# Query and key halves of a three-phase attention kernel, through DRAM into head order

## The reference

```python
x = x + 0.5 * ffn(norm(x))        # softmax attention and experts
x = x + linear_attention(norm(x)) # elu + 1 features, causal
x = x + 0.5 * ffn(norm(x))        # the same weights again

def ffn(x):                       # 16 heads of 8, 8 experts, top 2
    h = layernorm(x, ln1);  q, k, v = h @ wq, h @ wk, h @ wv
    scores = where(causal, q @ k.T, -inf)
    x = x + softmax(scores / sqrt(8)) @ v @ wo + bo
    h = layernorm(x, ln2);  top 2 of h @ gate_w, softmax over the two
    return x + sum over the two of weight * (silu(h @ w1) * (h @ w2)) @ w3

def linear_attention(x):
    q, k = elu(x @ Wq.T) + 1, elu(x @ Wk.T) + 1;  v = x @ Wv.T
    kv, ks = cumsum(k outer v), cumsum(k)         # per head, over tokens
    return (q . kv / max(q . ks, 1e-6)) @ Wo.T
```

## Time and profile before

| | |
|---|---|
| median of 3 runs | 1413.6 us (1412.59 to 1418.59) |
| the profiled execution | 1418.66 us, span 1416.9 us |
| mean granted clock of TensorE | 0.912 of full speed |
| busy in the span | TensorE 77%, VectorE 79%, ScalarE 59%, GpSimd 39% |
| SyncE's queue | 72.68 MB, 17.7% of the time of 16 DMA engines |

### The profile page before, as it was taken

How to read it: one execution, slowest core, us unless ns; L and a number is a source line. 1 busy time by engine, 2 the same in 40 slices (tenths; PEclk the granted TensorE clock), 3 DMA queues, 4 the chain that set the end, 5 groups by cost and what they waited for, 6 DMA issues and landing times.

```text
span 1416.9 us, 37025 instructions
## 1 busy us (share of the span) xinstructions
PE 1085.8 (77%) x12412; PEld 819.6 (58%) x12412; DVE 1115.8 (79%) x2411; ACT 839.7 (59%) x1311; POOL 548.4 (39%) x681
## 2 busy tenths in 40 slices
PE   4688888888854998476877868989888888549980
PEld 3566666666643666255655546857666666436660
DVE  6868889999965887677577767779999999658875
ACT  2457777777843555244656544668777787535550
POOL 6620255555563666201000004002555555636661
PEclk9899999999966999688999987999999999769995
DMA  8911111111102332201033310011111111023326
GB/s 292 412 48 38 43 46 49 51 43 51 53 20 61 86 90 69 82 30 34 7 77 79 79 43 19 0 28 45 50 49 45 51 53 47 26 57 88 87 72 187
DMA packets 124880, 98.71 MB, mean 70 GB/s; under 512 B 41584, under 2 KB 116848, under 8 KB 124784
## 3 DMA queue, kind: packets, MB, share of 16 engines
q1 hardware_dynamic: 103216, 72.68, 17.7%
q0 software_dynamic: 9088, 18.76, 4.0%
q10 hardware_dynamic: 12480, 6.02, 1.5%
HBM read 24.61 MB, written 40.94 MB: 46 GB/s over the span
## 4 chain that ended last, share of the span: by engine, by line
DVE 29%; PE 24%; issue 20%; ACT 9%; POOL 6%; DMA 6%; SPq 3%; DVEq 1%; ACTq 1%; POOLq 0%
DVE negm L1058 6%; PE banks L311 4%; POOL ys L1464 4%; SPq L1552 3%; PE banks L293 3%; DVE p_lo L1277 2%; DMA kst<-k_all 2%; DVE negm L1062 2%; ACT pf L866 2%; DVE pf L1284 2%; DVE x_all L1017 2%; PE banks L434 2%; ACT p_hi L732 2%; PE banks L430 2%; PE banks L466 2%
## 5 line engine op out<-in xcount | busy, mean ns | idle before, releaser
L715 ACT ACTIVATE pf<-banks 128x1536 f32<-128x1536 f32 x128 | 185.7, 1451 | 121.0 <-PE banks L455 119.9
L1070 DVE TENSOR_TENSOR p_lo<-pf,p_hi 128x1536 f16<-128x1536 f32 x128 | 223.9, 1749 | 3.2 <-ACT p_hi L732 3.0
L1464 POOL DMA_INDIRECT ys<-q_all,dest x156 | 151.4, 970 | 115.8 <-ACT q_all L872 90.9
L732 ACT CAST p_hi<-pf 128x1536 f16<-128x1536 f32 x128 | 188.7, 1474 | 2.0
L1415 POOL DMA_INDIRECT xs<-n_all,slot x128 | 164.7, 1287 | 54.9 <-issue 37.6
L1058 DVE TENSOR_REDUCE negm<-banks 128x4 f16<-128x1024 f32 x128 | 156.0, 1219 | 28.7 <-PE banks L434 20.3
L1441 POOL TENSOR_SCALAR rs<-mv 128x2 f32<-128x2 f32 x32 | 44.3, 1385 | 346.0 <-DVE mv L1113 295.3
L455 PEld LDWEIGHTS banks<-ident,negm 128*128 128x128 f16 x1536 | 119.7, 99 | 78.1 <-issue 4.4
L455 PE MATMUL banks<-ident,negm 128*128 128x128 f16 x1536 | 150.1, 221 | 0.0
L448 PE MATMUL banks<-qst,kst 128*128 128x512 f16 x384 | 148.1, 386 | 2.1 <-ACT pf L715 2.1
L434 PE MATMUL banks<-kst,qst 128*128 128x128 f16 x1536 | 129.7, 221 | 0.0
(11 more groups left out here) (206 smaller groups left out, 2820.9 us busy)
## 6 DMA issues: line engine op xcount, KB each, us to landing
xs<-qst SPq DMA_DIRECT2D x20, 975.0 KB, 25.4
qst<-q_all SPq DMA_DIRECT2D x384, 32.0 KB
q_all<-xs SPq DMA_DIRECT2D x78, 130.0 KB
kst<-k_all SPq DMA_DIRECT2D x66, 128.0 KB
pf<-ys SPq DMA_DIRECT2D x32, 256.0 KB, 3.0
v_hl<-v_all SPq DMA_DIRECT2D x66, 68.0 KB, 2.1
kst<-k_all ACTq DMA_DIRECT2D x30, 128.0 KB
ys<-q_all,dest POOLq DMA_INDIRECT x156
```

What stands on the lines that cost most here:

```text
L715: nc.scalar.activation(pf[:, g % 2, :, :, :].rearrange(flat), banks_t[:, :, :].rearrange("p a b -> p (a b)"), ACT.Exp, scale=HD ** -0.5).t ...
L732: nc.scalar.copy(p_hi[:, g % 2, :, :, :].rearrange(flat), pf[:, g % 2, :, :, :].rearrange(flat))\
L1070: nc.vector.tensor_tensor(lo, pf[:, g % 2, :, :, :].rearrange(flat), hi, ALU.subtract)\
L1464: nc.gpsimd.indirect_dma_start(ys, bass.IndirectOffsetOnAxis(ap=dest[:, t % YB, h:h + 1], axis=0), y_out[:, t % YB, h, :], None).then_inc( ...
```

## The change

The selection matrices, `front_spread`, its evacuations, `q_all` and `k_all` are removed. A DRAM tensor `qk_d` takes their place, with the rows in head order. SyncE stores each batch's high and low halves to it in six DMAs of 64 KB, as soon as `qk_low` is done; `qk_hi` and `qk_lo` have three buffers, and ScalarE's `qk_high` waits until the store of three batches before has landed. `load` brings a whole batch back in six DMAs (four of queries, one of keys, one of values) into one of three places (`RB = 3`) of `qst`, `kst` and `v_hl`. TensorE waits for a batch as a whole (`batch_in`), and SyncE loads batch b when batch b - 3 is finished.

The order in SyncE's queue is: all 16 stores of a phase, then the loads of batches 0, 1, 2, then in the first phase w3 (`load_w3`) and the clears (`clear_rows`, from a new buffer `zeros`), then the other loads. In the linear phase loads of the experts' results are placed between the stores, and ScalarE issues no DMA any more.

`xn`, `ht` and the three PSUM banks of the front have two buffers; transposes run two batches ahead and normalisation three. VectorE now waits for the reciprocal roots of the second group ahead of step 0, and takes the third group's statistics ahead of step 1. The first memsets of VectorE stand ahead of its first statistics. The fronts are written out in place of loops, and TensorE's attention loop runs three batches a pass. The score matmuls contract over `KR = 96` rows.

```diff
+RB = 3
+KR = 3 * GH * HD
+STORES = 16 * 6
+LOADS = 16 * 6
...
-        xn = sb("xn", [P, T, P])
-        ht = sb("ht", [P, T * P])
-        q_all = sb("q_all", [P, B, G, T * P], F16)
-        k_all = sb("k_all", [P, B, G, T * P], F16)
+        xn = sb("xn", [P, 2, T, P])
+        ht = sb("ht", [P, 2, T * P])
...
+        kst = sb("kst", [P, RB, G, T * P], F16)
+        qst = sb("qst", [P, RB, G, GH, T * P], F16)
+        v_hl = sb("v_hl", [P, RB, T, H, VC], F16)
+        zeros = sb("zeros", [P, ZR * RW])
...
+        qk_d = nc.dram_tensor("qk_d", [B, 2, G * GH, 3, HD, T * P], F16).ap()
...
+            def front_step(ph, b):
                 front_v(ph, b)
                 front_qk(ph, b)
+                if not ph["soft"] and b >= 2:
+                    front_carry(ph, b - 2, b % 2)
+                if b + 2 < B:
+                    front_turn(ph, b + 2)
+                if not ph["soft"] and b >= 1:
+                    front_keys(ph, b - 1, (b - 1) % 2)
+                    front_state(ph, b - 1, (b - 1) % 2)
...
+            def batch_in(ph, place):
+
+                ring, n = place
+                pe.wait_ge(ph["loaded"][ring], LOADS * (used(ph, ring, n) + 1))
...
+            def qk_high(ph, b):
+                ring = b % RB
+                hi = qk_hi[:, ring, :, :].rearrange("p a b -> p (a b)")
+                if b >= RB:
+                    sc.wait_ge(ph["stored"][ring], STORES * used(ph, ring, b // RB))
...
-            def front_constants():
-
-                c.link(nc.gpsimd.memset(sel[:, :, :, :, :, :, :], 0.0))
...
+            def store(ph, b):
+
+                ring = b % RB
+                sy.wait_ge(ph["qk_out"], b + 1)
+                for k, parts in ((0, ((0, qk_hi), (1, qk_hi), (2, qk_lo))),
+                                 (1, ((0, qk_hi), (1, qk_lo), (2, qk_hi)))):
+                    for r, src in parts:
+                        sy.dma_start(qk_d[b, k, :, r, :, :], src[:, ring, k, :]).then_inc(ph["stored"][ring], 16)
+
+            def load(ph, b):
+
+                ring, n = b % RB, b // RB
+                if b >= RB:
+                    sy.wait_ge(ph["turned"], ph["n"] * (S * B) + (b - RB + 1) * S)
+                    sy.wait_ge(ph["pv_done"], ph["n"] * (S * B) + (b - RB + 1) * S)
+                sy.wait_ge(ph["v_out"], ph["n"] * B + b + 1)
+                sy.wait_ge(ph["stored"][ring], STORES * (used(ph, ring, n) + 1))
                 for j in range(GH):
+                    rows = slice(KR // GH * j, KR // GH * (j + 1))
+                    sy.dma_start(qst[rows, ring, :, j, :],
+                                 qk_d[b, 0].rearrange("(g j) r d m -> j (r d) g m", j=GH)[j])\
+                        .then_inc(ph["loaded"][ring], 16)
+                sy.dma_start(kst[0:KR, ring, :, :], qk_d[b, 1].rearrange("(g j) r d m -> j (r d) g m", j=GH))\
+                    .then_inc(ph["loaded"][ring], 16)
+                sy.dma_start(v_hl[:, ring, :, :, :], v_all[:, b, :, :, :]).then_inc(ph["loaded"][ring], 16)
...
             def attention(ph):
+                if ph is phases[0]:
+                    sy.wait_ge(cleared, 1)
+                for b in range(B):
+                    store(ph, b)
+                    if not ph["soft"] and b % 2 and b + 7 < B:
+                        load_y(mixtures[0], b + 7)
+                        load_y(mixtures[0], b + 8)
+                for b in range(B):
+                    load(ph, b)
+                    if ph is phases[0] and b == RB - 1:
+                        load_w3()
+                        clear_rows()
```

More of the change, by code:

```diff
@@ L250, in apart, with used, at_batch, at_loop @@
             eng.sem_inc(passed, 1)
+        def used(ph, ring, n):
+            return ph["n"] * len(range(ring, B, RB)) + n
+        def at_batch(b):
+            return lambda d: ((b + d) % RB, (b + d) // RB)
+        def at_loop(i, n):
+            return lambda d: ((4 + n + d) % RB, i + (4 + n + d) // RB)
         def fill_no(ph, b, name):
@@ L552, in attention @@
                     back_gate(ph, B - 2)
[L553 removed]
+                values(ph, B - 1, S - 1, at(0))
                 back_turn(ph, B - 1)
@@ L630, in _, with qk_exp @@
         def _(sc):
-            def spread_out(ph, b, which=range(3)):
-                for n in which:
-                    dst, part = (q_all, k_all)[n // 2], n % 2
-                    sc.wait_ge(ph["spread_done"], ph["n"] * (4 * B) + 4 * b + n + 1)
-                    nc.scalar.copy(dst[:, b, 2 * part:2 * part + 2, :].rearrange("p a b -> p (a b)"),
-                                   psum[3 + n][:, :]).then_inc(ph["act_spread"], 1)
-            def qk_exp(ph, b, buf):
+            def qk_exp(ph, b):
@@ L703, in front @@
                     keys_out(ph, B - 1, 1)
-                spread_out(ph, B - 1)
-                if not ph["soft"]:
                     carry_out(ph, B - 1)
+                for ring in range(RB):
+                    sc.wait_ge(ph["stored"][ring], STORES * used(ph, ring, len(range(ring, B, RB))))
             def exps(ph, b, g, place=0):
@@ L791, in gates_out, with iteration @@
                     .then_inc(ph["emptied"], 1)
-            def iteration(ph, b, place=4, last=False, turn=0):
+            def iteration(ph, b, place=4, turn=0):
                 for g in range(S):
@@ L805, in iteration @@
                     exps(ph, b, g, (turn + g) % 3)
-                    if not ph["soft"] and g % 2 and not last:
-                        next_k(ph, b, g // 2)
                     if ph["soft"] and g == 1 and place > 1:
@@ L819, in iteration @@
                         pv_read(ph, b, 0)
-                        if not ph["soft"] and not last:
-                            next_v(ph, b, 0)
             def attention(ph):
@@ L996, in front @@
                 front_stats(ph, 1)
-                front_step(ph, 0, 0, first=True)
-                front_stats(ph, 2)
                 ve.wait_ge(ph["rstd"], 2)
-                for start, end in ((1, 5), (5, B - 3)):
-                    if start > 1:
+                for b in range(B):
+                    if b == 1:
+                        front_stats(ph, 2)
+                    if b == 4:
                         ve.wait_ge(ph["rstd"], 3)
-                    with ve.Fori(start, end, 2) as b:
-                        front_step(ph, b, 1)
-                        front_step(ph, b + 1, 0)
-                front_step(ph, B - 3, 1)
-                front_step(ph, B - 2, 0, before_last=True)
-                front_step(ph, B - 1, 1, last=True)
-                spread_out(ph, B - 1)
+                    front_step(ph, b)
             def add(m, b, c):
@@ new lines, in clear_rows, with load_w3 @@
+            def clear_rows():
+                sy.wait_ge(cleared, 1)
+                for n in range(ZN):
+                    rows = min(ZR, ROWS // P - ZR * n)
+                    sy.dma_start(xs[n * ZR * P:n * ZR * P + rows * P, :].rearrange("(p r) d -> p (r d)", p=P),
+                                 zeros[:, 0:rows * RW]).then_inc(blank, 16)
+            def load_w3():
+                sy.wait_ge(w_split, 2)
+                for c in range(HC):
+                    for e0 in (0, 4):
+                        sy.dma_start(stage3[:, e0:e0 + 4, c, :],
+                                     w3[e0:e0 + 4, c * P:(c + 1) * P, :].rearrange("e h d -> h e d")).then_inc(w3_in, 16)
@@ L1621, in _ @@
                 if n == 0:
-                    for b in range(B):
+                    for b in range(8):
                         load_y(mixtures[0], b)
```

366 lines of the change are left out of this document (122 added, 244 removed).

## The result

The changed kernel takes 1457.3 us in the median of 4 runs (1456.5 to 1460.9), the kernel before 1413.1 in the same session (4 runs, 1412.6 to 1418.6): 1.031 times as long, 95% interval 1.028 to 1.034. The forecast was 1403, its range 1386 to 1424: wrong in sign, and outside the range by 33 us.

A forecast was written before the change was run, and what follows sets the result against it. VectorE was taken to pace the softmax attentions and TensorE the fronts, with SyncE's issues the third front's new pace. First phase +7, second -14.3 - 2, third +3.9 - 5 gave -10.4 us: 1403, range 1386 to 1424.

The forecast's parts named there:

- The price of a store: SyncE's issue of one 64 KB store taken as 0.49 us start to start, 2.94 us for a batch's six.
- The two bounds: Issue prices on SyncE: 0.47 us for a store from SBUF to DRAM, 0.64 for a copy from SBUF to SBUF.
- Rival 1: Store and load issues are dearer: at 0.64 us each, 27 us more, 1430 in all; chance 0.2.
- the two soft fronts: First front's end at 98.7 us against 99.2, nothing won; third front 3.9 us longer.
- the order of the starts, the memsets, the new tail: Soft fronts: roots awaited before step 0; clearing memset 3 x 1.76 us; first load issued in 2.94 us, landing 2.2 later.
- gain from the loads ahead: Linear attention: fewer waits for queries win between nothing and some 5 us, taken as -2.
- The second front: Without spreads a step takes 4.4 us and a pair 12 to 13; front -14.3 us, range -17 to -5.
- rival 3: Second front doesn't speed up: TensorE falls to its lower clock, a step stays at 5 us; +10, 1413; chance 0.2.
- The first attention: Batch 3's load waits behind w3 and clears, TensorE stands 12.5 us, 3 won back; first phase +7.
- the drain: First attention: 21 MB of clears drain at 420 GB/s, 50 us, ahead of batch 3's load, landing at 157.5.
- The rival that the clears don't hold batch 3: First attention: clears drain in time or batch 3's packets pass them; 12.5 us less, 1390 to 1394; chance 0.15.
- The third attention: Softmax attention of the third phase: with loads ahead, waits for keys and a slow batch 0 shrink; -5 us.

The follow-up runs named there:

- e2: The changed kernel, still six stores a batch, with DRAM blocks ordered (head, dim, block) so a store's rows lie at one fixed distance: 1433.4 us, 1.016 of before.
- e9: Changed kernel with three stores a batch, plus three unread matmuls before the linear attention's wait for the context, nothing moved: 1394.9 us, 0.985 of before.
- e5: Changed kernel with three stores a batch, the linear attention's score matmuls contracting over all 128 rows again: 1407.6 us, 0.995 of before.
- e10: The kernel before the change, with the fourth group's products moved ahead of the wait for the context in the linear attention: 1399.5 us, 0.990 of before.
- e12: Changed kernel with three stores a batch, clears split, products ahead of context, and 14 unread matmuls in second-front steps waiting for `pair_in`: 1367.3 us, 0.966 of before.
- e8: Changed kernel with three stores a batch, the 21 clears issued in three parts behind the loads of batches 2, 3 and 4: 1399.5 us, 0.987 of before.
- e6: Changed kernel with three stores a batch, the fourth group's products moved ahead of the linear attention's wait for the context: 1383.9 us, 0.977 of before.
- e7: Changed kernel with three stores a batch, plus seven unread matmuls in every batch of the second front: 1419.0 us, 1.003 of before.

## Why the prediction was wrong

**The price of a store.** "I take 0.49 from start to start, since the store row is the same kind of transfer": this step failed. The store of the earlier trace rows and the clear of the earlier trace rows have the same kind of source and destination, but another pattern. These stores scatter 128 SBUF rows over (head, dim) and paid 0.64; e2 took one level out of the pattern and paid 0.475. The two bounds were not read alike: 0.64 is from start to start, 0.47 an issue without its gap. That the stores came out at the upper one to the digit is luck as far as the runs show: none tells why they cost what a copy from SBUF to SBUF costs. Rival 1 with its 27 us measured 24 (1457.3 less 1433.4). Its chance of 0.2 was low, since the row nearest in kind was one whose pattern I hadn't compared. Where e2 put the price back, the two soft fronts came out to 0.7 us, and the last store of the third front was issued 70.5 us after its start, where 70.6 were worked out. So the rest of their working (the order of the starts, the memsets, the new tail) was right.

**The linear attention.** The forecast looked for a gain from the loads ahead, between "nothing and some 5 us", and took -2. It was +12.4, outside those bounds. The waits for queries did go. But idle time that lies in the shadow of another chain isn't removed when its wait is removed: it moved to the next wait, the context's, and became one halt of 1.35 us, behind which the clock fell (e9: 16 us; e5 rules out the rows). Some 1.6 of the 12.4 us are the entry at the lower clock (e10). The failed step is that the prediction gave the clock no term here: I had read the earlier trace rows for the clock in the fronts and never asked it of the linear attention, where it stood at 0.95 with 3 of 16 batches already falling. No rival had this mechanism, and that is the larger fault: the first was a misjudged size.

**The second front.** The mechanism was right: the step no longer waits for spreads, and a pair takes 14.1 us instead of 15.4. The size was off: 12 to 13 was forecast, from 4.4 us a step; 14.1 a pair is 5.2 a step, what the prediction had named for the lower clock. TensorE after the change, one pair:

```profile
637.47 0.63 PE L328 MATMUL bank_mx<-pos,pf 128*128 128x144 f32 x2 [4.20 <-DVE pos L889]
...
640.58 1.06 PE L298 MATMUL banks<-w_v,ht 128*128 128x128 f32 x4
641.43 1.91 PE L307 MATMUL banks<-ht,w_qk 128*128 128x256 f32 x4
643.14 0.69 PE L328 MATMUL bank_mx<-pos,pf 128*128 128x144 f32 x2
...
646.30 1.03 PE L307 MATMUL banks<-ht,w_qk 128*128 128x256 f32 x4
651.63 0.85 PE L328 MATMUL bank_mx<-pos,pf 128*128 128x144 f32 x2 [4.30 <-DVE pos L889]
```

The halt of 4.20 us is followed by projections of 1.91 us, against 1.03 in the other step. This is rival 3, at a granted clock of 0.67. e12 fills that halt and the front takes 112.2 us; the forecast's own was 128.1 - 14.3 = 113.8.

**The first attention.** Batch 3 waited behind w3 and the clears as worked out, and TensorE stood for 12.7 us, 12.5 by the forecast; the stage got +11.4 where +7 was forecast. The dear stores are not the reason: e2, without them, has the same 487.1 us. Counted from the phase's first score matmul, the load of batch 3 landed at 62.4 us and not at 58.8, and from batch 3 on the stage won 2.9 us, 3 by the forecast. The mis-sized term is the drain: from the first clear's issue to that landing 57.5 us passed, at 385 GB/s in the mean, where 53.1 were worked out from 420; w3's 2.1 MB had been given no drain time. That TensorE's stall still came out as forecast is luck: batch 3 was also wanted later, at 50.2 us and not at 46.3, which the 3.9 us of the slowed subtractions could explain; no run parts them. e8 gives 13.4 us for the stall. The rival that the clears don't hold batch 3 falls.

**The third attention** won 3.1 us of 5. The fronts' rests came as forecast in e2. The softmax attentions past their fourth batch hardly moved: in the first phase 19.2 us a batch before and 19.0 after, from one second read of products to the next.

**In sum**, by the stages of the profiled executions: the span came out at 1459.1 us, 52.6 above the 1406.5 of the forecast. The price of the stores has 25.9 of them (8.7 in the first front, 14.8 in the third, 2.4 in the second by e2), the linear attention 14.4, the rest of the second front 5.9 (the 14.3 forecast less the 8.4 that e2 won), the first attention 4.4, the third 1.9.

## What to carry to other kernels

When work moves to a queue, price the issue by a row with the same access pattern, not only the same kind of memory; if there is none, give the dear bound more weight when the whole sum turns on it. Then ask of every wait that goes: is the engine's idle time gone, or is it now in one piece at the next wait, and what does TensorE's granted clock do behind a piece of that length? Where it falls, useful work put into the halt is worth most (e6), and even work that nothing reads is worth its place (e9), as long as it stands only where the engine would stand still (e7 against e12).

## What the runs showed of the hardware

- What SyncE pays to issue a store depended on the pattern in DRAM and not on the bytes: the same 64 KB from 128 SBUF rows took 0.60 us with the destination walked as (head, dim, row) and 0.43 with rows at one fixed distance; 128 KB as two rows per partition took 0.47 to 0.48. ScalarE's queue had the same price (0.62) for the dear form.
- TensorE's granted clock seemed to respond to how its idle time is divided and not to the sum alone: 1.74 us a batch in two halts went with 0.95, 1.63 us mostly in one with 0.84, and with three matmuls in that one (0.96 us idle, 0.68 the longest) it was 0.98. With 96 or 128 contraction rows it was 0.84 and 0.86.
- Behind a queue full of large transfers the issuing engine is held up: a load of queries took SyncE 0.44 us from start to start normally and 2.3 behind the 21 clears.
- A VectorE subtraction with two SBUF inputs took 3.14 and 4.24 us beside GpSimd operations that read SBUF, and 1.74 without them.
